# Adapted residual ahead of the transposes, and both scatters behind the low half of h1, in a pipelined two-layer-block kernel

## The reference, cut to what matters

```python
# block 1: y = LayerNorm(x + net[condition](x)) * gamma + beta
out_nr  = gelu(x @ w1_nr  + b1_nr)  @ w2_nr  + b2_nr          # 256 -> 256 -> 256
out_tsr = gelu(x @ w1_tsr + b1_tsr) @ w2_tsr + b2_tsr
out_sr  = gelu(gelu(x @ w1_sr + b1_sr) @ w2_sr + b2_sr) @ w3_sr + b3_sr   # 256 -> 512 -> 256 -> 256
# block 2: 64 units, expert and embedding of the sequence's domain
h = gelu(y @ down_W.T + down_b)
h = h @ expert_W[dom].T + expert_b[dom] + domain_emb[dom]
out = LayerNorm(h @ up_W.T + up_b + y) * ln_gamma + ln_beta
```

## Time and profile before

| what | us |
|---|---|
| median of 3 runs | 267.83 |
| lowest and highest | 267.12, 269.02 |
| the profiled execution | 267.34 |
| its span on the core | 265.5 |
| TensorE busy | 248.2 (93%) |
| VectorE busy | 210.6 (79%) |
| ScalarE busy | 192.1 (72%) |
| GpSimd busy | 175.6 (66%) |

### The profile page before, as it was taken

One profiled execution on the slowest core, in us unless ns is written; L12 is line 12 of the kernel. 1 busy time (PEld: TensorE's weight loads), 2 busy tenths in 40 slices (PEclk: granted clock), 3 DMA queues, 4 the chain that ended last, 5 costly groups with the idle time before them and its releaser, 6 DMA issues.

```text
span 265.5 us, 8050 instructions
## 1 busy us (share of the span) xinstructions
PE 248.2 (93%) x2114; PEld 219.8 (83%) x2115; DVE 210.6 (79%) x717; ACT 192.1 (72%) x450; POOL 175.6 (66%) x188
## 2 busy tenths in 40 slices
PE   7998999999999997899999999999999999999960
PEld 6698898999899987698998889999889999987640
DVE  6769643563945847688999999999989999999893
ACT  3578479578686685686788887878888787878640
POOL 3134474373767757587887888888788888878451
PEclk9999999999999999999999999999999999999995
DMA  6372011011121121123323333332333333332315
GB/s 197 93 263 63 13 42 38 8 44 39 33 55 53 45 59 40 40 76 83 99 79 99 86 88 93 89 99 80 98 86 90 91 89 99 85 94 56 74 42 122
DMA packets 41639, 20.71 MB, mean 78 GB/s; under 512 B 37430, under 2 KB 39180, under 8 KB 41613
## 3 DMA queue, kind: packets, MB, share of 16 engines
q1 hardware_dynamic: 37625, 12.10, 18.8%
q0 software_dynamic: 2592, 7.08, 7.6%
q10 hardware_dynamic: 1396, 1.19, 1.7%
HBM read 11.69 MB, written 8.65 MB: 77 GB/s over the span
## 4 chain that ended last, share of the span: by engine, by line
PE 65%; DVE 12%; issue 11%; POOL 6%; DVEq 2%; ACT 2%; DMA 1%; POOLq 0%; ACTq 0%
PE ps_h L1093 18%; PE ps_z L1161 11%; PE ps_u L1213 8%; PE ps_z L1166 5%; PE ps_z L1128 5%; PE ps_t L1183 5%; PE ps_d L1226 4%; PE ps_u L1128 4%; POOL h_lo L482 3%; POOL rs L489 2%; DVE o L769 2%; DVE st L713 2%; DVE st L690 1%; DVE nm L706 1%; PE ps_u L1050 1%
## 5 line engine op out<-in xcount | busy, mean ns | idle before, releaser
L482 POOL TENSOR_TENSOR h_lo<-h,h_hi 128x256 fp32r<-128x256 f32 (+1 forms) x75 | 71.5, 953 | 43.1 <-ACT h L907 41.9
L914 ACT ACTIVATE zn<-ps_z,nm,rs 128x256 f32<-128x256 f32 x66 | 33.7, 561 | 29.4 <-DVE nm L706 28.9
L489 POOL TENSOR_TENSOR rs<-ve,minus_half 128x4 f32<-128x4 f32 (+1 forms) x38 | 38.2, 1006 | 24.8 <-DVE ve L702 24.5
L690 DVE BATCH_NORM_STATS2 st<-ps_z 128x6 f32<-128x256 f32 x66 | 24.8, 416 | 32.1 <-PE ps_z L1166 32.0
L907 ACT ACTIVATE h_hi<-ps_h,per_feature_sb 128x256 fp32r<-128x256 f32 x84 | 38.6, 491 | 10.4 <-issue 4.9
L907 ACT ACTIVATE h<-ps_h,per_feature_sb 128x256 f32<-128x256 f32 x84 | 38.8, 497 | 0.0
L508 POOL DMA_INDIRECT out<-o,out_rows_now x27 | 34.7, 1284 | 4.9 <-issue 4.9
L769 DVE SCALAR_TENSOR_TENSOR o<-n,rs,per_feature_sb 128x256 f32<-128x256 f32 x64 | 36.5, 608 | 0.3
L941 ACT ACTIVATE yt<-ps_t,per_feature_sb 128x256 f32<-128x256 f32 x66 | 34.0, 572 | 2.7 <-PE ps_t L1183 2.4
L1213 PE MATMUL ps_u<-tables,stack 65*64 x132 | 35.6, 392 | 0.3 <-ACT stack L925 0.3
L1161 PE MATMUL ps_z<-last_hi,h_hi 128*128 (+1 forms) x132 | 35.6, 304 | 0.0
(11 more groups left out here) (150 smaller groups left out, 648.3 us busy)
## 6 DMA issues: line engine op xcount, KB each, us to landing
x<-in_x_feat SPq DMA_DIRECT2D x130, 64.0 KB
out<-o SPq DMA_DIRECT2D x18, 64.0 KB, 2.0
out<-o,out_rows_now POOLq DMA_INDIRECT x54
last_sb<-in_last_w SPq DMA_DIRECT2D x1, 768.0 KB, 4.8
w_sr_sb<-in_w_sr SPq DMA_DIRECT2D x1, 512.0 KB, 3.3
w_sr_sb<-in_w_sr ACTq DMA_DIRECT2D x1, 512.0 KB, 4.4
w_two_sb<-in_w_two SPq DMA_DIRECT2D x1, 512.0 KB, 5.4
out<-o ACTq DMA_DIRECT2D x6, 64.0 KB, 2.3
```

The source lines that it names most:

```text
L482: pool.tensor_tensor(dst, full, high.bitcast(F32), ALU.subtract).then_inc(ready, 1)
L489: pool.tensor_tensor(RS[p][:, norms, :], VE[p][:, norms, :], half_of_two[:, norms, :], ALU.pow).then_inc(rstd, 1)
L914: ins = act.activation(ZN[:, t, :], ZP[p][:, t, :], ACT.Identity, bias=NM[p][:, t:t + 1], scale=RS[p][:, 0, t:t + 1])
```

## The change

It has two parts.

**A, two-layer steps on TensorE.** `adapter` puts the adapted residual of slot g-2 (four transposes into `ps_u`) ahead of the transposes of slot g-1. Before, the order was transposes, input residual, adapted residual, expert products; after, it is adapted residual, transposes, input residual, expert products. The waits of `adapted_residual` (on the centring of slot g-4 and on `yt` of slot g-2) move with it.

**B, steps where slot g+1 is three-layer, on GpSimd.** The scatter of tile 1 moves from between the power and the low part of h1's second half to behind it, next to the scatter of tile 0. In the other steps the order on GpSimd stays as it was; both scatters now stand once, behind the branch.

```diff
@@ gpsimd
+            def store(g, where):
+                if where in (MAIN, LAST2):
+                    store_tile1(g - 4, p)
+                    store_tile0(g - 4, p)
...
                 with pool.If(g + 1 < b_sr):
                     low(h1l[:, 0:2, :], h1[:, 0:2, :], h1h[:, 0:2, :], h0_full, h0_lo, g + 1)
                     powers(g, i, p, where)
-                    if where in (MAIN, LAST2):
-                        store_tile1(g - 4, p)
                     low(h1l[:, 2:4, :], h1[:, 2:4, :], h1h[:, 2:4, :], h1_full, h1_lo, g + 1)
                 with pool.Else():
...
                     for slot in on_slot(g, -1, where):
                         low(h2l[:, 1, :], h2[:, 1, :], h2h[:, 1, :], h1_full, h1_lo, g + 1)
-                    if where in (MAIN, LAST2):
-                        store_tile1(g - 4, p)
-                if where in (MAIN, LAST2):
-                    store_tile0(g - 4, p)
+                store(g, where)
@@ tensor
             def adapter(g, p, where):
                 at = [tables_of(slot) for slot in on_slot(g, 2, where)]
+                for slot in on_slot(g, 2, where):
+                    adapted_residual(slot, p, where)
                 for slot in on_slot(g, 1, where):
                     transposes(slot, where)
                 input_residual(g, 1 - p, where)
                 for slot in on_slot(g, 2, where):
-                    expert(slot, p, where, at[0])
+                    expert_products(slot, p, where, at[0])
```

## The result

The changed kernel takes 270.46 us (median of 8 runs, 268.57 to 271.87) against 268.04 us (8 runs, 267.09 to 269.02) for the kernel before: a ratio of 1.0096, 95% interval 1.0066 to 1.0125. It is slower, by about 1%. The forecast was 264.8 us and its range ended at 266.7, so the forecast was wrong and the range missed the time. The profiled execution took 268.57 us with a span of 266.8 us, against 267.34 and 265.5 before. It is the fastest of the changed kernel's eight, so its trace shows 1.2 us of a loss that is 2.4 us by the medians.

The account below looks back on a forecast made before the run. TensorE, busy 93% of the span, was taken as the bound, idling in three-layer steps with late `x`. Profiled 267.34 us minus 2.86 (part B) and 0 (part A) gave 264.48, shifted 0.3 to 264.8 us; range 263.6 to 266.7.

Parts of the forecast that it names:

- Part B, -2.86 us: Three-layer steps with scatters, g = 4 to 7: `h_lo` directly behind the power lets `x` come earlier, saving 2.86 us.
- g = 4 to 6: First three three-layer steps with scatters: the input residual no longer waits for `x`, saving 0.75, 0.59 and 0.59 us.
- g = 7: Last three-layer step with scatters: `x` comes 0.93 us earlier, saving that; a wait of about 0.9 us for `x` remains.
- Part A, 0 us: Two-layer steps: TensorE has no idle time to win, and transposes 0.44 us later fit the slack, so 0 us.
- 0.05 us a step (1.2 us) as the bad end of the range: Two-layer steps: worst loss allowed for part A in the range, though passing on all 0.44 us would cost 10.1 us.
- Rival 2: Two-layer steps: later transposes delay `yt`, TensorE waits at the down projection; 266.0 or 267.3 us; chance 8%.
- 1: Three-layer steps with scatters: a scatter by itself blocks DVE's `o`, 0.50 us more per step, 269.3 us; chance 5%.
- 3: Three-layer steps: scatters beside `o`, `x` and table copies delay `x`, leaving 1.4 us of gain, 266.2 us; chance 12%.
- 4: Two-layer steps: part A gains 0.05 us a step where TensorE changes product kind, 1.2 us, 263.6 us; chance 5%.

Follow-up runs that it names:

- without the spare wait: The changed kernel without the adapted residual's wait for `yt`: 263.93 us on chip 3, 270.57 us on chip 4.
- B alone with its spare wait: Kernel before with only the scatter move, plus a long-fulfilled wait for `yt` ahead of the transposes: 263.95 us, ratio 0.9911.
- A alone: Kernel before with only the new TensorE order, GpSimd's scatters left where they were: 273.56 us, ratio 1.0213.
- T, U, Z, X: Changed kernel with TensorE's order transposes, adapted residual, input residual, expert products: 271.09 us, ratio 1.0159.
- B alone: Kernel before with only the scatter move on GpSimd, TensorE's order as before: 265.07 us, ratio 0.9908.

## Why the prediction was wrong

- **Part B, -2.86 us: right, and 0.2 too large.** The four steps give back 2.66 us. g = 4 to 6 take 10.12, 10.11 and 10.10 us (forecast for the first two 10.11 and 10.07); g = 7 keeps a 0.76 us wait for `x` (forecast 0.9) and gives 0.83 us instead of 0.93. Alone it measured 265.07 against 267.25 us on a chip that loses, 2.2 us, with all counts on time.
- **Part A, 0 us: wrong, and this step failed:** "`ps_t` is ready 0.44 us later, and so is the buffer that SP's next loads wait for; ACT reads those only in the next step ... The cost is 0 by these rows." I followed both moved results to their readers and found slack at each, 0.16 us at the down projection. That slack was real: on chip 3 the twenty steps take 116.22 us with part A (and without the spare wait), as many as in the kernel before (116.40), and the kernel takes 263.93 us, as much as B alone with its spare wait (263.95). What I didn't follow was the moved issue of the loads against the transfers of another queue. I asked when their data was wanted, not what they would now run beside. What stood in its place: TensorE's counts of the first layer come up to 1.7 us late in 15 of 21 steps, and the twenty steps take 4.69 us more in the profiled pair. The late counts vanish when either the loads or the scatters are taken away; that it is the moved issue which brings them is the likely reading, not a shown one.
- **"The bounds: ... 0.05 us a step (1.2 us) as the bad end of the range": too narrow.** I had written the full bound myself, 0.44 us in each of 23 steps, 10.1 us, and then let a slack worked out from one undisturbed step set the end of the range. A alone measured +2.1%, 6.3 us; the whole of it lay within the bound and outside the range.
- **Rival 2** had the sign and the place (TensorE waits at L1227 for `yt`) but the wrong mechanism: T, U, Z, X keeps the transposes where they were and loses as much. Its price has a slip too: 0.12 us a step is 264.8 + 2.8 = 267.6 us by the sum that gives 266.0 for 0.05, not 267.3.
- **Rivals 1, 3 and 4:** 1 is out by the `o` row at 0.87 us, 3 by the three steps without a wait for `x`, and 4 by the steps of 5.80 us that part A keeps where nothing is late.
- The sign was on the page. One two-layer step of the kernel before took 6.16 us where the changed kernel takes 5.76, with a wait of 1.51 us for a matmul long done. I read steps that were typical and took the stretch as 23 of the same.

What stays open: why it came on chips 1, 2, 4 and 6 and not on 3 and 5, whether that is the chip or the time, and what holds the counts. That both transfers (with their issue) are needed is shown on chip 6. Another rival is untested: each run on record has a span and a granted clock, so it was recorded as it ran, and where counts are late many of its events are missing, so no run shows whether they are late when nothing is recorded. Against it stands only that without the loads events are missing as well (1,467 against 1,850) and no count is late. The distance of 0 to 0.25 us is a correlation over 210 steps, its bands were drawn after looking at these same steps, and the steps of one trace depend on each other; a scatter or a load shifted by 0.4 us with all else in place was tried on chip 5 only, which has no late counts, and so it isn't shown as a cause. The changed kernel itself did not run on chip 3 or 5; what it would take there is inferred from the one without the spare wait, which equals it on chip 4.

The version to keep is B alone: 0.9908 [0.9887, 0.9929] on a chip that loses, and with a spare wait 0.9911 [0.9887, 0.9935] on one that doesn't. Part A gains nothing on either.

## What to carry to other kernels

Of a moved instruction, follow not only who reads its result but which transfers its result sets off, and lay their issue against those of the other queues: here a shift of 0.43 us that no reader should have felt went with a loss of about 2%. Before calling a long row of steps uniform, look for the one that isn't, and for an engine idle behind work that was already done. And run the control beside the cure, on the same chip: without it, a spare wait would have been blamed that has nothing to do with it.

## What the runs showed of the hardware

- A semaphore count of TensorE can come up to 1.74 us after its matmul, while the array goes on without a gap; the waiting engine's row then says "remote" or names a matmul that was over (1.58 us, 1.51 us).
- It comes in some places or at some times only: chips 1, 2, 4 and 6 show it, 3 and 5 don't, and the same program took 263.93 us on one and 270.57 us on another. The kernel before took 266.45 to 268.04 us in all six groups, so its own time doesn't tell the two kinds apart.
- The traces tell: with both transfers they hold 2,311 to 2,594 landing events on the first kind and 3,415 to 3,490 on the second. With the scatters left out both kinds hold 2,650; with the loads left out it is 1,467 against 1,850. So the two kinds differ in the events only where the scatters run.
- A scatter on GpSimd alone doesn't hold up an instruction of DVE with two SBUF inputs: 0.87 us beside it, as the earlier trace rows had it.
